# Attention and feed-forward block on one Trainium2 core: queries of tiles 1 to 3 loaded with features on partitions and centred by VectorE, in place of TensorE turning centred rows

## What is computed

```python
B=8, S=256, D=256                      # x, ctx_1024: (8, 256, 256); mask: (8, 256), 1 keeps a key, 0 hides it
def attention(q, kv, mask):            # _L0_xattn_ref
    scores = jnp.einsum('bqd,bkd->bqk', q, kv) / math.sqrt(256)
    scores = jnp.where(causal, -inf, scores)          # keys after the query
    scores = jnp.where(mask == 0, -inf, scores)
    return jnp.einsum('bqk,bkd->bqd', jax.nn.softmax(scores, axis=-1), kv)
def tlin(x, w, s): return jnp.einsum('bsi,oi->bso', x, w) * s        # w holds -1, 0 or 1
def ffn(x):                            # hidden width 1024
    h = silu(tlin(x, w1_w, w1_s)) * tlin(x, w2_w, w2_s)
    h = gelu(tlin(h, h1_w, h1_s)); h = gelu(tlin(h, h2_w, h2_s))     # the exact gelu
    return tlin(h, w3_w, w3_s)
x = x + attention(layernorm(x), ctx_1024, mask)       # layernorm: (x - mean) / sqrt(var + 1e-5)
return x + ffn(layernorm(x))
```

## Time and profile before

| | |
|---|---|
| time, median of 3 runs | 377.39 us |
| the three runs | 375.11, 377.39 and 377.93 us |
| time of the profiled execution | 376.71 us |
| span of the profiled execution | 374.6 us |
| granted TensorE clock in it | 1.00 of full speed |
| PE busy | 364.7 us (97%) |
| PEld busy | 306.8 us (82%) |
| DVE busy | 176.9 us (47%) |
| ACT busy | 149.3 us (40%) |
| POOL busy | 28.5 us (8%) |

### The profile page before, as it was taken

How to read it: one execution, slowest core, us unless ns; L and a number is a source line. 1 busy time by engine, 2 the same in 40 slices (tenths; PEclk the granted TensorE clock), 3 DMA queues, 4 the chain that set the end, 5 groups by cost and what they waited for, 6 DMA issues and landing times.

```text
span 374.6 us, 4879 instructions
## 1 busy us (share of the span) xinstructions
PE 364.7 (97%) x1797; PEld 306.8 (82%) x1797; DVE 176.9 (47%) x406; ACT 149.3 (40%) x252; POOL 28.5 (8%) x50
## 2 busy tenths in 40 slices
PE   8898999999999999999998999999999999999996
PEld 5676888888898888888888888888889888888886
DVE  2747652334565745234564665232456563232324
ACT  3678766593134632262130653235113473122120
POOL 7300031000100022000010004000010000000000
PEclk9999999999999999999999999999999999999999
DMA  7989998981411000000141000000000100000001
GB/s 260 335 288 366 380 401 281 317 274 70 173 40 46 3 2 2 2 0 3 59 139 60 2 1 3 0 2 3 2 0 30 32 3 2 2 2 2 2 2 58
DMA packets 10499, 34.15 MB, mean 91 GB/s; under 512 B 1522, under 2 KB 4468, under 8 KB 10100
## 3 DMA queue, kind: packets, MB, share of 16 engines
q1 hardware_dynamic: 10448, 33.45, 24.9%
q10 hardware_dynamic: 4, 0.00, 0.0%
HBM read 31.34 MB, written 13.63 MB: 120 GB/s over the span
## 4 chain that ended last, share of the span: by engine, by line
PE 93%; issue 2%; ACT 1%; DVE 1%; POOL 1%; DMA 1%; DVEq 0%; ACTq 0%
PE ring L928 62%; PE ring L907 14%; PE ring L947 8%; PE att L858 2%; PE att L877 2%; PE att L848 1%; DMA mask<-in_mask 1%; ACT scaled L391 1%; PE ring L1073 1%; ACT gate L468 1%; PE att L866 1%; PE ring L1055 0%; ACT h_hi L458 0%; PE ring L1092 0%; POOL rstd L338 0%
## 5 line engine op out<-in xcount | busy, mean ns | idle before, releaser
L928 PE MATMUL ring<-h_hi,weights 128*128 128x512 f32 x512 | 201.5, 394 | 0.1
L928 PE MATMUL ring<-h_lo,weights 128*128 128x512 f32 x512 | 199.5, 390 | 0.0
L928 PEld LDWEIGHTS ring<-h_hi,weights 128*128 128x128 f32 x512 | 96.2, 188 | 19.9 <-issue 0.2
L928 PEld LDWEIGHTS ring<-h_lo,weights 128*128 128x128 f32 x512 | 96.2, 188 | 19.7
L480 ACT ACTIVATE act<-ring,scales 128x512 f32<-128x512 f32 x64 | 44.1, 689 | 155.8 <-PE ring L928 155.8
L716 DVE CAST h_hi<-act 128x512 fp32r<-128x512 f32 x64 | 27.3, 427 | 147.9 <-ACT act L480 134.1
L610 DVE TENSOR_TENSOR h_lo<-act,h_hi 128x512 fp32r<-128x512 f32 x96 | 66.2, 689 | 2.6
L907 PE MATMUL ring<-xn_hi,weights 128*128 128x512 f32 x112 | 43.7, 390 | 1.5 <-issue 1.5
L907 PE MATMUL ring<-xn_lo,weights 128*128 128x512 f32 x112 | 43.6, 389 | 0.0
L468 ACT ACTIVATE gate<-ring,scales 128x512 f32<-128x512 f32 x32 | 22.1, 690 | 37.6 <-PE ring L907 37.6
L703 DVE SCALAR_TENSOR_TENSOR act<-ring,scales,gate 128x512 f32<-128x512 f32 x32 | 24.0, 751 | 21.5 <-PE ring L907 17.0
(11 more groups left out here) (119 smaller groups left out, 243.5 us busy)
## 6 DMA issues: line engine op xcount, KB each, us to landing
weights_staged<-in_weights SPq DMA_DIRECT2D x22, 512.0 KB, 7.0
weights<-weights_staged SPq DMA_DIRECT2D x22, 512.0 KB, 5.6
x_in<-in_x SPq DMA_DIRECT2D x8, 256.0 KB, 2.9
ctx_cols<-in_ctx_cols SPq DMA_DIRECT2D x8, 256.0 KB, 4.3
ctx_rows<-in_ctx_rows SPq DMA_DIRECT2D x4, 512.0 KB, 6.3
out_dram<-residual SPq DMA_DIRECT2D x16, 128.0 KB, 2.2
mask<-in_mask SPq DMA_DIRECT2D x3, 256.0 KB
gate<-in_weights SPq DMA_DIRECT2D x1, 512.0 KB, 5.2
```

What stands on the lines that cost most here:

```text
L928: ins = nc.tensor.matmul(bank[:], w, part[:, k].bitcast(dt), start=(k == 0 and part is h_hi[src]), stop=(k == HC - 1 and part is h_lo[src]))
```

## The change

The input `x` is given a second time, in a layout with features on partitions (`in_x_cols`). For tiles 1 to 3 SP loads it straight into `q_cols` (one DMA of 512 KB). POOL, which makes the reciprocal deviations, first multiplies the row means by 1/16 into a new small tile. SP stores these 512 numbers to DRAM (16 bytes from each partition), waits until the store has landed, and loads them back spread over all 128 partitions into the first half of `work` (256 KB written). DVE then makes the queries in place, four instructions over 128x256: x times 1/16 less the mean. The centred rows in `work`, PE's eight products on them per tile and ACT's two copies are gone. Tile 0 makes its queries as before. The second `turn_rows`, of the normalised rows, stays.

```diff
+    means_d = nc.dram_tensor("means", [TILES, P, ROWS], F32).ap()
+        mean_cols = work[:, 0:TOK].rearrange("p (t b q) -> p b q t", b=PAIR, q=2)
...
+            def load_query_cols(t):
+
+                sp.dma_start(q_cols[:], x_cols_d[t].rearrange("b p c t -> p b c t")).then_inc(x_cols_in, 16)
+
+            def spread_means(t):
+
+                sp.wait_ge(mean_made, t)
+                sp.dma_start(means_d[t], mean_scaled[:]).then_inc(mean_stored, 16)
+                sp.wait_ge(mean_stored, 16 * t)
+                sp.dma_start(work[:, 0:TOK], means_d[t].rearrange("p r -> (p r)").partition_broadcast(P)
+                             ).then_inc(mean_loaded, 16)
+
             def load_next(t):
 
                 sp.wait_ge(x_attn_done, ROWS * t)
@@ -246,6 +264,7 @@
                 load_keys(t)
                 load_mask(t)
                 load_values(t)
+                load_query_cols(t)
...
                     load_keys(1)
                     load_mask(1)
                     load_values(1)
+                    load_query_cols(1)
+                if n == FLAG_PIECES[HID2A][0] + 1:
+                    spread_means(1)
             for n in range(2):
                 load_piece(n)
             for t in range(TILES - 2):
                 load_next(t + 2)
                 store(t)
+                spread_means(t + 2)
...
                 pool.wait_ge(moments, ROWS * (2 * (t - 1) + norm + 1))
+                if not norm:
+                    nc.gpsimd.tensor_scalar(mean_scaled[:], mean_var[:, :, 0], SCALE, 0.0, ALU.mult, ALU.add
+                                            ).then_inc(mean_made, 1)
                 rstd_of(slice(0, ROWS)).then_inc(rstd_ready, 1)
...
-            def evacuate_q(t):
-                for b in range(PAIR):
-                    act.wait_ge(q_turned, PAIR * (t - 1) + b + 1)
-                    nc.scalar.activation(turned[:, b * 512:(b + 1) * 512], att[b][:], ACT.Copy, scale=-SCALE
-                                         ).then_inc(q_evacuated, 1)
...
-                        if more and (layer, c) == (0, HID1_CHUNKS[1][1] - 1):
-                            evacuate_q(t + 1)
...
+            def centre(t, b):
+
+                dve.wait_ge(x_cols_in, 16 * t)
+                dve.wait_ge(mean_loaded, 16 * t)
+                for c in range(EC):
+                    cols = q_cols[:, b, c].rearrange("p (q t) -> p q t", q=2)
+                    nc.vector.scalar_tensor_tensor(out=cols, in0=cols, scalar=SCALE, in1=mean_cols[:, b],
+                                                   op0=ALU.mult, op1=ALU.subtract).then_inc(q_centred, 1)
...
-                        if at == (0, 2):
-                            for r in range(ROWS):
-                                normalise(t + 1, 0, x_in, r)
+                        if at == (0, 6):
+                            for b in range(PAIR):
+                                centre(t + 1, b)
...
-                    pe.wait_ge(q_evacuated, PAIR * (t - 1) + b + 1)
+                    pe.wait_ge(q_centred, PAIR * EC * (t - 1) + EC * (b + 1))
...
                 hid1(HID1B, 4)
-                pe.wait_ge(flag_ready, HID1C + 1)
-                turn_rows(1, 0, q_turned)
                 hid1(HID1C, 5, 6)
-                pe.wait_ge(q_evacuated, PAIR)
                 sum_flag(HID2A)
...
                 hidden_segment(0, (3, 5))
-                if more:
-                    turn_rows(t + 1, 0, q_turned)
                 hidden_segment(0, (5, 8))
```

More of the change, by code:

```diff
@@ L107, in xattn_ffn @@
         inv_sum = sb("inv_sum", [P, ROWS])
+        mean_scaled = sb("mean_scaled", [P, ROWS])
         xn = work[:].rearrange("p (r d) -> p r d", r=ROWS)
@@ L139, in xattn_ffn @@
         ctx_rows_in = sem("ctx_rows_in")
+        x_cols_in = sem("x_cols_in")
+        mean_made = sem("mean_made")
+        mean_stored = sem("mean_stored")
+        mean_loaded = sem("mean_loaded")
         mask_loaded = sem("mask_loaded")
@@ L171, in xattn_ffn @@
         result_done = sem("result_done")
-        q_turned = sem("q_turned")
+        q_centred = sem("q_centred")
         scores_done = sem("scores_done")
@@ L840, in _, with turn_rows @@
         def _(pe):
-            def turn_rows(t, norm, done):
+            def turn_rows(t):
                 for b in range(PAIR):
                     for r in (2 * b, 2 * b + 1):
-                        pe.wait_ge(xn_ready, ROWS * (2 * (t - 1) + norm) + r + 1)
+                        pe.wait_ge(xn_ready, ROWS * (t - 1) + r + 1)
                         for c in range(EC):
@@ L848, in turn_rows @@
                             ins = nc.tensor.transpose(att[b][:, at:at + P], xn[:, r, c * P:(c + 1) * P], ident[:])
-                    ins.then_inc(done, 1)
+                    ins.then_inc(xn_turned, 1)
             def scores(t):
```

20 lines of the change are left out of this document (9 added, 11 removed).

## The result

The changed kernel takes 379.76 us in the median of nine runs (378.15 to 382.21), against 376.91 (375.00 to 377.93) for the kernel before on the same chips: a ratio of 1.0095, 95% interval 1.0062 to 1.0128 (it follows the mean times, 380.02 and 376.44; the medians alone give 1.0076). The forecast was 375.9 with a range of 373.8 to 378.6. The change costs 2.9 us where 0.8 was to be gained, and the measured time lies above the range.

What follows compares the result with a forecast made beforehand. PE was taken to bound nearly the whole span. Tile 0 at +0.9 us (2.6/3 gained, 1.75 lost) and tiles 1 and 2 at -1.74 gave -0.8, so 375.9 us from 376.71; range 373.8 to 378.6.

Steps and rivals of the forecast that it cites:

- Eight products for each of three tiles: 2.6 us.: PE, three places: the turning products removed save 0.87 us each, 2.6 us off PE's path.
- Added in tiles 1 and 2, off the path: Tiles 1 and 2: the means' round trip, query columns and DVE's four instructions delay nothing; price 0.
- the bound with 0.95: DVE's centring: were each instruction 0.95 us, twice as long, PE would wait 0.1 at the scores.
- Behind copy 15 the store lands at 61.4 plus 0.3: 61.7.: SP's queue, tile 0: the store of the means, issued at 52.3, lands at 61.7, just behind copy 15.
- By now the queue is empty. Load 14 lands at 65.7.: SP's queue, tile 0: load 14, issued at 62.2 behind the load of the means, lands 3.6 us later than before.
- The bound of 66.7: SP's queue, tile 0: other estimate of load 14's landing, 4.5 us behind its issue as before.
- Flag HID2A's sum: PE waits 1.75.: PE, tile 0, between chunks 6 and 7: waits 1.75 us for ACT's test, goes on 0.9 later than before.
- The wait is so long that PE's clock falls: Rival, tile 0: two chunks at 1.2 GHz cost 7 us, total about 383; chance 0.05.
- What is late next: Later pieces in tile 0, load 20 to flag LAST: extra wait of PE taken as 0, upper bound 0.9.
- The second rival: Tile 0: SP's standstill for the store costs more than the products save; 377.8 to 378.6 us; chance 0.27.
- The first rival: Tile 0: the store does not stand behind the copies, lands in 2.2 us; total 374.2; chance 0.17.
- The fourth: Rival: DVE's strided instructions take over 0.9 us each and PE waits at the scores; 379.1 at 1.1 each; chance 0.06.

Runs made afterwards that it cites:

- after_third: The changed kernel, unaltered, run again for a third trace; 379.27 us.
- act_store: The changed kernel with the store of tile 1's means issued on ACT's queue, behind its test of piece 11; 374.22 us, 0.994 of the kernel before.
- experiment 5: The kernel before with twelve 8-column products added at PE's start, 378.34 us (second trace 378.13), and the kernel before unaltered again, 375.23 us.
- store_ahead: The changed kernel with the store of tile 1's means issued on SP between load 13 and copy 15; 377.15 us, 0.999 of the kernel before.
- no_standstill: The changed kernel with tile 1's means stored one load and copy earlier and loaded behind load 14 and copy 16; 374.14 us, 0.992 of the kernel before.
- both_moved: The changed kernel with tile 1's means stored behind load 12, their load and the query columns behind load 14; 374.7 us, 0.994 of the kernel before.
- experiment 6: The changed kernel unaltered twice more, 381.73 and 379.27 us, and with twelve 8-column products added at PE's start, 376.57 us.
- tile1_turned: The changed kernel with tile 1's queries made as before (turned by PE, no new DMA in tile 0); 373.57 us, 0.991 of the kernel before.
- experiment 3: The changed kernel with the store of tile 1's means on ACT's queue, 374.22 us, or on SP ahead of copy 15, 377.15 us.
- after_shifted: The changed kernel with twelve 8-column products added at PE's start; 376.57 us, 1.003 of the kernel before.

## Why the prediction was wrong, point by point

Of the three traces of the changed kernel that of after_third, 379.27 us, is the nearest to the median and is taken for the accounts. Against the profiled execution of before it has S -0.45, A +6.07 and R -3.02, together +2.6. A is the wait of 4.19, chunk 7 at half clock for the most part (5.83 - 3.78 = 2.05), 0.87 from the start of the flag sum to chunk 7 in place of 0.12 (+0.75), and the turning saved (-0.87): 6.12. Not all of the 2.8 behind the wait is the clock. In act_store, behind a wait of 1.00 and at full clock, the same stretch from the flag sum to the end of chunk 7 takes 0.8 more than before (0.77 to chunk 7, and 3.92 for it). So 0.8 is PE's restart behind any such wait, with the gelu that stands behind the test, and 2.0 is the clock.

- **"Eight products for each of three tiles: 2.6 us."** Right: 0.87 less at each place.
- **"Added in tiles 1 and 2, off the path", price 0.** Right. One instruction of DVE takes 0.60 to 0.64 instead of 0.475, and nothing waits for it there, as the bound with 0.95 had said. R gained 1.3 more than forecast, 1.1 of it the idle time of the earlier trace rows that is gone; experiment 5 puts it down to where PE's code stands. This was not in the sum, and it hides part of the loss.
- **"Behind copy 15 the store lands at 61.4 plus 0.3: 61.7."** Right, by its number in after_third (61.7, copy 15 at 61.5) and by its reason: in every trace the store lands with what was issued just ahead of it, in store_ahead with load 13, 1.3 us sooner. In the other two traces of the changed kernel the stream ran late and it landed at 64.2.
- **"By now the queue is empty. Load 14 lands at 65.7."** Here the step fails that sets the size. The term that was too small is the load of the means. I took 2.5 for it, from a 256 KB load of rows, and 1.25 for the piece behind it, 3.5 from load 14's issue, and named the 4.5 of the earlier trace rows as the other end. The load of the means took 4.7 in after_third and 4.4 in the other two traces, and even on idle DMA engines, in tiles 1 and 2, it takes 3.5 to 4.1; load 14 then followed 1.3 to 1.4 behind it, as forecast. In after_third it landed at 67.8, 5.7 after its issue at 62.09. In no_standstill, with the load of the means behind it, load 14 took 3.6. Why the load that spreads 2 KB over all partitions takes longer than one of rows with as many bytes written is not shown. The bound of 66.7 was passed by one microsecond even with the store on time.
- **"Flag HID2A's sum: PE waits 1.75."** It waited 4.2 to 5.0. Of the 2.4 missing in after_third, load 14 is 2.1, which is the 2.2 by which the load of the means was longer. The rest is PE, which arrived at 64.8 where I had it at 65.1. The moment of PE and that of the load were both read from one execution; the three traces of the changed kernel have PE at 64.8 to 66.3 and the test's end at 68.9 to 71.2.
- **"The wait is so long that PE's clock falls", 0.05.** The chance was far too small and the price too large. Nothing in the trace of before allowed a bound for the wait that brings this on; the one long wait it has (1.09 us) lasted less than the forecast wait of 1.75, and so it did not speak against the clock falling. The clock fell in every run of the changed kernel. By the account above it cost 2.0 us in after_third and 2.8 in the first trace, not the 7 of two whole chunks. PE's restart behind a wait, 0.8, was not in the sum at all.
- **What is late next: 0 at flag LAST.** Right: no trace has a wait there.
- **The second rival** (SP stands still, later pieces are late) had the mechanism and with 0.27 too little weight. "It decides from the point where load 14 lands later than 66.6": it did, in all three traces (67.8 to 70.0). But it put the delay into the store, 2.2 behind copy 15 where 0.1 to 0.2 was measured, and its 377.8 to 378.6 lie below the result, since it has no clock in them. The first rival's store in 2.2 us or less exists only in tiles 1 and 2. The fixed cost that the prediction quotes for it stands in the Trainium skill, "DMA: Bandwidth & Descriptors", section "Anatomy of one DMA", for DMAs that GpSimd issues; SP issues these, and the 1.4 to 1.7 of tiles 1 and 2 is this case's number. The fourth, PE waiting at the scores, showed in both_moved alone, and for another reason.

From the forecast to the measurement: 375.9 + 2.4 (wait) + 2.0 (clock) + 0.8 (restart behind the wait) - 1.3 (R) - 0.45 (S) = 379.35, against 379.27. The first three, 5.2 us, have one cause, the late load, and the 1.3 of R and an early start (luck, both) masked part of them. The size of the loss is itself one of a race: with twelve tiny products at PE's start (experiment 6) the same change gave the forecast's time in seven of ten executions.

The version that comes out best is tile1_turned: queries with features on partitions only where the DMA queue is idle, in tiles 1 and 2, and PE's turning in tile 0.

## What to carry to other kernels

A queue that stands in the middle of a stream to wait for a tiny DMA pays three times: the tiny DMA lands no sooner than what was issued ahead of it, the stream drains meanwhile, and the load that depended on it stands ahead of the next piece; issue the first half early and the second half later, or change only the tiles in which the queue is idle. When a forecast puts a new wait of a microsecond or two on PE, price the loss of its clock as well and not as a rare case, and set the two arrivals against each other by their spread over executions, not by one trace. Idle time of the kind "issue" can vanish or appear through any edit ahead of it, so the part of a gain that comes from there is not the edit's.

## What the runs showed of the hardware

- A store of 2 KB takes 1.4 to 1.7 us on idle DMA engines and 8.1 to 12.1 amid weight loads, on another engine's queue too (8.1). It landed within 0.2 us of the transfer issued just ahead of it in all six traces of the table in experiment 3.
- A load that spreads 2 KB over 128 partitions (256 KB written) takes 3.5 to 4.1 us on idle DMA engines (tiles 1 and 2 of the first and third trace) and 4.4 to 4.7 in tile 0. A 512 KB load right behind it needs 5.3 to 5.8 us to land in the changed kernel's traces and after_shifted, against 4.5 and 3.9 for the same piece in the two traces of before.
- After 4.2 and 5.0 us of idleness PE ran at 1.2 GHz for 4.9 and 6.9 us (from 68.99 to 73.85 in after_third, from 71.25 to 78.11 in the first trace). A wait of 1.24 us brought this on in part in one trace, and one of 1.45 did not in another.
- Twelve tiny products at PE's start moved the changed kernel's median by -3.2 us; on the kernel before the same edit gave a ratio of 1.003 (1.000 to 1.006).
- `scalar_tensor_tensor` over 128x256 in 4-byte numbers takes 602 to 636 ns where all operands are in SBUF and one is strided, against 475 with one in PSUM.
